# First transfers of a perceiver block in another order on two queues

## What is computed

```python
x = x + cross_attention(layernorm(x), context, mask, Wq, Wk, Wv, Wo)   # scores masked before the softmax
x = x + local_attention(layernorm(x), Wq, bq, Wk, bk, Wv, bv)          # window of 5
x = x + experts(layernorm(x), Wr, br, W1, b1, W2, b2, W3, b3)          # argmax over 8 experts, gelu
```

## Time and profile before

| | |
|---|---|
| median of 3 runs | 704.46 us (704.05 to 704.51) |
| the profiled execution | 707.72 us |
| its span, first to last instruction | 706.0 us |
| granted TensorE clock, mean | 0.992 |
| PE, PEld | 686.0 us (97%), 582.1 us (82%) |
| DVE, ACT, POOL | 473.8 us (67%), 450.7 us (64%), 437.7 us (62%) |
| HBM read and written | 67.30 MB and 7.27 MB, 106 GB/s over the span |

### The profile page before, as it was taken

The page is one execution under the profiler, slowest core; times in us unless marked ns, Lnnn a source line. Parts: engine busy times, 40 slices in busy tenths (PEclk is TensorE's granted clock), DMA queues, the critical chain, the costliest instruction groups (busy, mean ns, idle before and its releaser), DMA issues.

```text
span 706.0 us, 26647 instructions
## 1 busy us (share of the span) xinstructions
PE 686.0 (97%) x9297; PEld 582.1 (82%) x9298; DVE 473.8 (67%) x1456; ACT 450.7 (64%) x1071; POOL 437.7 (62%) x596
## 2 busy tenths in 40 slices
PE   7999999999999999999999968999999999999996
PEld 6888888888888888888888756888888888888885
DVE  4467677777777777777798878999961991259001
ACT  4656666666766766666666644575757576666663
POOL 6475665655656565656555663677766776767553
PEclk9999999999999999999999997999999999999999
DMA  7432233333323333343458334239033541272100
GB/s 214 118 89 78 75 76 96 91 88 82 97 67 80 102 90 78 81 97 80 94 136 268 99 109 169 90 100 330 25 106 112 176 147 45 82 229 69 40 7 1
DMA packets 56178, 74.35 MB, mean 105 GB/s; under 512 B 6589, under 2 KB 41950, under 8 KB 56128
## 3 DMA queue, kind: packets, MB, share of 16 engines
q1 hardware_dynamic: 49792, 60.63, 31.2%
q0 software_dynamic: 2992, 8.26, 3.8%
q10 hardware_dynamic: 3344, 4.80, 1.9%
HBM read 67.30 MB, written 7.27 MB: 106 GB/s over the span
## 4 chain that ended last, share of the span: by engine, by line
PE 93%; DVE 2%; DMA 1%; issue 1%; POOL 1%; ACT 1%; SPq 0%; POOLq 0%; ACTq 0%; DVEq 0%
PE ps_s L2046 18%; PE ps_kv L1623 12%; PE ps_kv L1631 11%; PE ps_p L1709 8%; PE ps_o L1695 6%; PE ps_s L1642 6%; PE ps_p L1994 5%; PE ps_kv L1994 4%; PE ps_o L2060 4%; PE ps_s L2025 3%; PE ps_m L1828 2%; PE ps_m L1774 2%; PE ps_m L1747 2%; PE ps_m L1832 2%; PE ps_s L2054 1%
## 5 line engine op out<-in xcount | busy, mean ns | idle before, releaser
L877 ACT ACTIVATE prob<-prob,neg_max 128x257 f32<-128x257 f32 x256 | 111.2, 501 | 42.2 <-DVE neg_max L1122 40.6
L1122 DVE CUSTOM_DVE_ANT_0 prob<-ps_s,mask_add 128x257 f32<-128x257 f32 x256 | 94.7, 421 | 64.3 <-PE ps_s L1642 64.2
L1582 DVE CAST w<-w_raw 128x512 fp32r<-128x512 f32 x94 | 68.1, 725 | 57.1 <-DMA w_raw<-in_L_ffn_W_dram 57.1
L1585 DVE TENSOR_TENSOR w<-w_raw,w 128x512 fp32r<-128x512 f32 x112 | 103.1, 923 | 3.6
L685 POOL TENSOR_TENSOR ctx_parts<-ctx_raw,ctx_parts 128x512 fp32r<-128x512 f32 x64 | 82.9, 1295 | 23.8 <-ACT ctx_parts L872 21.9
L2046 PE MATMUL ps_s<-w,h_hi 128*128 x368 | 90.5, 397 | 0.0
L1631 PE MATMUL ps_kv<-wkv_hi,ctx_parts 128*128 128x256 f32 x512 | 84.6, 293 | 0.2 <-ACT kT L881 0.2
L1623 PE MATMUL ps_kv<-ctx_parts,wkv_hi 128*128 128x256 f32 x512 | 84.2, 292 | 0.3 <-POOL ctx_parts L685 0.2
L885 ACT COPY v<-ps_kv 128x512 f32<-128x512 f32 x64 | 37.5, 586 | 70.3 <-PE ps_kv L1631 70.3
L698 POOL COPY last_prob<-prob 128x4 f32<-128x4 f32 x64 | 12.3, 192 | 112.1 <-ACT prob L877 108.4
L813 POOL TENSOR_TENSOR h_lo<-h,h_hi 128x512 fp32r<-128x512 f32 x46 | 64.2, 1397 | 27.6 <-ACT h_hi L1017 21.4
(11 more groups left out here) (307 smaller groups left out, 1513.6 us busy)
## 6 DMA issues: line engine op xcount, KB each, us to landing
w_raw<-in_L_ffn_W_dram SPq DMA_DIRECT2D x24, 1024.0 KB, 7.2
ctx_raw<-in_ctx_turned_dram SPq DMA_DIRECT2D x63, 256.0 KB, 3.5
mask_add<-mask_dram SPq DMA_DIRECT2D x64, 128.5 KB, 3.4
w_raw<-in_L_ffn_W_dram SPq DMA_DIRECT2D x8, 512.0 KB, 4.0
rows_dram<-x3n ACTq DMA_DIRECT2D x15, 256.0 KB, 4.3
xt<-in_x_dram SPq DMA_DIRECT2D x16, 128.0 KB, 2.1
xr<-in_x_dram SPq DMA_DIRECT2D x16, 128.0 KB, 2.3
slot_x<-rows_dram,slot_ids POOLq DMA_INDIRECT x23, 4.0
```

The costliest lines, as they stand in the source:

```text
L877: a.activation(prob[:, g, :], prob[:, g, :], ACT.Exp, bias=neg_max[:, g:g + 1], scale=-1.0).then_inc(exp_done, 1)
L1122: d.tensor_tensor_reduce(prob[:, r, :], ps_s[r][:, 0:J], mask_add[:, k, :], -(HD ** -0.5), 3.0e38, ALU.add, ALU.min, neg_max[:, r:r + 1]). ...
L1582: d.tensor_copy(w[:, b, HI, part], raw[:, b, part]).then_inc(rounded, 1)
L1585: last = d.tensor_tensor(w[:, b, LO, part], raw[:, b, part], f32(w[:, b, HI, part]), ALU.subtract)
```

## The change

Nothing is computed differently. On SP's queue the third transfer of Wk goes to ACT's queue, Wv and context 1 follow Wk at once, the store of the mask rows moves behind them, and all four mask loads move behind x's second tile and context 2. On ACT's queue context 0 comes first, `last_ctxT` second, then the third transfer of Wk, then Wq, and the mask's bytes last. On DVE the first tile is normalised before the mask rows are made, and the copy of the transposed rows (`middle(T, 0)`) comes ahead of the wait for Wk's rounding.

```diff
             sp.dma_start(wkv[0:C2, 0, 1, :], Wk[P:C, :]).then_inc(k_in, 16)
-            sp.dma_start(wkv[C2:P, 0, 1, :], Wk[P:C, :]).then_inc(k_in, 16)
-            sp.wait_ge(mask_done, 1)
-            sp.dma_start(mask_dram, mask_rows[:, :]).then_inc(mask_stored, 16)
             sp.dma_start(wkv[:, 1, 0, :], Wv[0:P, :]).then_inc(v_in, 16)
             sp.dma_start(wkv[0:C2, 1, 1, :], Wv[P:C, :]).then_inc(v_in, 16)
             sp.dma_start(wkv[C2:P, 1, 1, :], Wv[P:C, :]).then_inc(v_in, 16)
             load_ctx(0, 1)
-            sp.wait_ge(mask_stored, 16)
-            load_mask(0, 0)
+            sp.wait_ge(mask_done, 1)
+            sp.dma_start(mask_dram, mask_rows[:, :]).then_inc(mask_stored, 16)
             sp.wait_ge(xn1_done, 1)
             load_x(xt, 1, x_in)
             load_ctx(0, 2)
-            for b in range(1, BT):
+            sp.wait_ge(mask_stored, 16)
+            for b in range(BT):
                 load_mask(0, b)
             load_ctx(0, 3)
...
-                    act.dma_start(mask_bytes[:, :], mask).then_inc(mask_bytes_in, 16)
+                    act.dma_start(ctx_raw[:, 0, :, :], ctx_turned[0].rearrange("(c p) j -> p c j", p=P)).then_inc(ctx_in[0], 16)
                     act.dma_start(last_ctxT[:, :, :], last_turned.rearrange("(c p) b -> p c b", p=P)).then_inc(last_in, 16)
-                    act.dma_start(ctx_raw[:, 0, :, :], ctx_turned[0].rearrange("(c p) j -> p c j", p=P)).then_inc(ctx_in[0], 16)
+                    act.dma_start(wkv[C2:P, 0, 1, :], Wk[P:C, :]).then_inc(k_in, 16)
                     act.wait_ge(consts, 1)
                     a.activation(row_inv[:, 0:1], neg_half[:, :], ACT.Exp, bias=neg_half[:, 0:1])
                     act.dma_start(wq[:, :, :], Wq.rearrange("(c p) n -> p c n", p=P)).then_inc(wq_in, 16)
+                    act.dma_start(mask_bytes[:, :], mask).then_inc(mask_bytes_in, 16)
...
                     moments_of(0, 0, xt[:, :])
+                    normalise(0, 0, xt[:, :], xn1[:, :], xn1_done)
                     dve.wait_ge(mask_bytes_in, 16)
                     d.tensor_scalar(mask_rows[:, :], mask_bytes[:, :], 1.0, -MASKED, ALU.subtract, ALU.mult).then_inc(mask_done, 1)
-                    normalise(0, 0, xt[:, :], xn1[:, :], xn1_done)
+                    middle(T, 0)
                     dve.wait_ge(wk_rounded, 1)
                     split_first_rows(0, wk_split)
-                    middle(T, 0)
                     split_last_rows(0, wk_split)
```

## The result

The changed kernel takes 707.02 us, the median of 8 runs (705.78 to 709.04), against 704.49 us (704.04 to 706.15) for the kernel before beside it: ratio 1.0036, 95% interval 1.0026 to 1.0045. It is **2.5 us slower**, 1.6 us above the upper end of the predicted range.

What follows compares the result with a forecast made beforehand. PE, with 93% of the chain, was taken as the bound, so keys(0)'s start counted: 0.5 us earlier, limited to 0.3 by a slow mask store, taken as 0.4. From 704.46 that gave about 704.1 us, range 702.9 to 705.4.

Steps and rivals of the forecast that it cites:

- Part 1 (context chain): Context 0 through POOL's shift and split to keys(0): moves up by 0.8 to 1.6 us and is not the last path.
- Part 2, M: Landing of the mask's bytes, last on ACT's queue: 6.5 us, with 6.2 to 7.0 as easily possible.
- My upper bound, Wq's own time: Latest landing of the mask's bytes: issue at 3.14 plus Wq's 4.5 us, giving 7.6.
- The hole in the earlier trace: DMA moved only 87 KB in microsecond 3 to 4; context 0 issued first fills it, worth 0.7 us.
- Part 2, normalise held by the shift: On DVE beside POOL's first shift: normalise ends 0.15 behind it, at 6.1 instead of 5.30.
- Part 2, PE's order: Clock matmuls end 1.65 us after normalise, at 7.75, then queries; keys(0) starts at 9.45 against 9.94, gain 0.5.
- Part 3 (round trip): Mask store issued at 6.8 instead of 3.92; first mask lands at 13.7, or 12.6 with a quick 2.4 us store.
- break-even of 14.0: Start of DVE's masked scores at which the later mask would use up the whole gain: 14.0 us.
- Part 4 (SP's later list): Later mask loads push SP's weights and biases back 1.85 us; last lands at 20.5, cost 0 to 0.2.
- Rival C: Mask's bytes land after POOL's split begins, so DVE's mask rows are held: loss 0.6 to 1.1 us, about 705.3; chance 0.21.
- the wait at L1799: Sign against the forecast: PE waiting at the local projections for local weights and biases; no size given.

Runs made afterwards that it cites:

- x1: The kernel before, with only the clamp on PE's 23 expert-number loads that every experiment carries; 704.86 us, ratio 0.9995.
- e2: The changed kernel with DVE's copy of the turned rows moved ahead of its wait for the mask's bytes; 706.13 us, ratio 1.0016.
- e4: The changed kernel with POOL's first context shift waiting until DVE has normalised the first rows; 706.64 us, ratio 1.0025.
- e11: The changed kernel with DVE's copy ahead of the mask and the mask's bytes issued later, behind ACT's wait for Wk; 706.78 us, ratio 1.0027.
- e12: The changed kernel with the mask's bytes third on ACT's queue, all of Wk on SP, and POOL's first shift waiting for normalise; 704.91 us, ratio 0.9999.
- e5: The changed kernel with 20 instead of 16 clock matmuls ahead of PE's transposes; 707.06 us, ratio 1.0036.
- e7: The changed kernel with POOL's first shift waiting for normalise, and local weights and biases issued before SP's wait for mask rows; 705.31 us, ratio 1.0002.
- e3b: The kernel before with DVE's new order alone, both queues as before; 707.28 us, ratio 1.0027.
- x0: The changed kernel with only the clamp on PE's 23 expert-number loads that every experiment carries; 706.51 us, ratio 1.0025.
- e8: The changed kernel with the mask's bytes first on ACT's queue and POOL's first shift waiting for normalise; 704.87 us, ratio 1.0000.
- e10: The kernel before with SP's new list alone, ACT's queue and DVE's order as before; 704.74 us, ratio 1.0001.
- e1: The changed kernel with the mask's bytes back in first place on ACT's queue, context 0 second; 704.63 us, ratio 1.0008.

## Why the prediction was wrong

The forecast was a gain of 0.4; measured is a loss of 2.5 by the medians and 1.9 at PE-local. From the rows of after, the 1.90 is 1.22 at keys(0), 0.32 between keys(0) and keys(1) (5.69 instead of 5.37), and 0.36 at the bias. The other 0.6 is not located; 0.38 of it is the difference between PE-local in the profile before and in x1, the same kernel, so it lies in the spread of single executions.

- **Part 1 (context chain)**: right in kind. The context landed at 3.86, before my 4.2, yet the shift started at 5.06 and the split ended at 8.48 (I had 7.9 to 8.1): Wk landed at 5.97, not by the 5.3 that I had made the condition, and ACT rounded it first. It was not the last path, as I said.
- **Part 2, M**: the term that went wrong first. I took 6.5 from the bytes ahead of it; it was 7.82 (7.1 to 8.0 in the other runs with this order). My upper bound, Wq's own time, was the right value: Wq took 4.9 and the mask's bytes 4.57. The hole in the earlier trace rows was filled (296 GB/s in the microsecond 3 to 4, from the row below). Context 1's 256 KB, which SP issued at 4.14 ahead of M, were missing from my bytes; that they took what the hole gave is my reading, no run leaves them out.

```profile
3.00:4.00 1.00, 1.00 (x7) 1.00 (x6) 0.61 (x2) 0.99 (x2) 0.00 (x0) 1.00 0.96 296
```

- **Part 2, normalise held by the shift**: right: 1.14 us where the earlier trace rows had 1.18, and its end at 6.24 where I had 6.1.
- **Part 2, PE's order**: the step that failed. I had the ten clock matmuls at 1.26 behind any start, since they took that before, and the queries at 1.13. They took 2.34 and 1.97 at half clock, 1.9 us more ahead of keys(0). Of this, 0.78 owes nothing to the change: x1, the unchanged kernel, shows 2.04, and my 1.26 was the value of an execution with early full clock. The other 1.1 (0.30 and 0.84) went along with PE's longer wait, which I had priced at its own length only. Nothing in my sum or rivals had either.
- **Part 3 (round trip)**: the store took the quick value (2.38), as half hoped, but started from 8.65 rather than 6.8. The masked scores at 14.60 are beyond the break-even of 14.0, yet PE was later still: the first mask landed at 14.41, and DVE's own work ahead of the scores ended at 14.48. In e2, e4, e11 and e12 DVE did wait for it, 0.7 to 2.1 us.
- **Part 4 (SP's later list)**: right in kind, mis-sized. I had the landing at 20.5 with a cost of at most 0.2. Issued at 17.49 instead of 15.1, it landed at 22.71. Of these 2.4 us at the issue, 0.75 are the mask loads (11.05 for 10.3: later mask rows, less the quicker store) and 1.54 the one issue of 2.01 us, where I had counted such issues at 0.47. Eight other runs of this list show one such issue at 0.9 to 1.54 ahead of the bias; in e12 none was above 0.71.
- **Rival C** named the mechanism that came: bytes behind the split's start, mask rows held to its end; and of what was to show me wrong, the wait at L1799 came. Its point, M above 6.6, was met with ease, its chance of 0.21 was too low with my own upper bound for M at 7.6, and its price of 0.6 to 1.1 left out the clock and the bias. The doubt it ended on, that an operation on 64 partitions may not be held, is settled: eight profiles show one held (0.70 to 1.13 us), each ending 0.15 behind POOL's operation.
- **Even the forecast's gain was no gain.** e12 reaches keys(0) at 9.05 and the time does not move. I had followed keys(0) as the only gate and not asked what keys(1) and the bias would do with an earlier one.

The held mask rows are also what the Trainium skill, page "SBUF — State Buffer", section "Who interferes with whom", leads one to expect: the one that issues first keeps the shared port pair for its whole instruction and the other is blocked. This case's rows agree (0.79 and 1.14 us beside POOL, 0.26 and 0.41 alone).

**What stays open.** PE-local plus 682.2 plus the 1.7 between span and time gives ten of the fourteen medians to 0.6 us. The medians of e5, e7 and e3b lie 1.1 to 1.9 above it and that of e4 0.8 below. Their executions spread by 1.6 to 3.7 us; whether half-clock stretches near 421 and 431 fall otherwise in them was not tried. And no run changes the clock without changing PE's waits or its luck: that PE's wait makes the clock late rests on the twelve traces and on pairs such as x0 and e4, one execution each; it is likely, and not shown by itself.

## What to carry to other kernels

Before a small transfer is put last on a queue, follow what hangs on it to its last user: here 16 KB of mask bytes gated a store, four loads and, through a queue's program order, a bias that PE needed 21 us into the kernel. Give the landing of a small transfer behind a big one about the big one's own time, not a share worked out from bytes: in the seven profiles with this order the mask's bytes took 3.9 to 4.8 us, 0.3 to 0.6 less than Wq just ahead of them. Price a wait on PE in an opening twice, with its length and with the work behind it at half clock, and take the clock of the opening from more than one execution: the same kernel had full clock at 4.65 in one and at 7.46 in another. That filler matmuls in the wait would help is not shown; e5's clock rose ahead of them. When two delays lie side by side, each hides the other, and only removing both shows either.

## What the runs showed of the hardware

- A wait of 0.9 to 1.1 us on PE, between 5.4 and 6.6 us into the kernel, went along with half clock until 10.2 to 11.3 us (five traces); waits of up to 0.5 went along with full clock by 7.8 at the latest (ten traces). In three of the ten (before, e8, e5) it had risen at 4.65 to 5.04, ahead of the wait; before and x1, the same kernel, had it at 4.65 and 7.46.
- A DVE tensor-scalar operation on uint8 input and 64 partitions is held by POOL's two-input operations just as the one on 128 partitions and float32 is, and by the shift too: in e12 the mask rows began at 5.81 beside it (5.46 to 6.50) and ended at 6.65.
- The store of 64 KB took 2.4 us with 42 to 45 GB/s moved meanwhile (x0, after) and 3.4 to 3.5 with 262 to 279 (before, e8, e10). A bias of 1 KB took 2.7 to 6.4 us: 2.7 with 181 and 220 GB/s (e10, e1), 6.4 with 277 (e12).
- Issuing one transfer on SP behind the mask's store took 0.43 to 0.60 us as a rule, and 0.9 to 2.0 us for one to three of them in each opening; in ten of the fifteen traces one of these was the first transfer of the local weights (L530 to L532).
